# Eight-layer transformer on one core: set-up, first normalisation and small projections written as one program

## What is computed

```python
def _layernorm(x, axis=-1, eps=1e-05):
    m = jnp.mean(x, axis=axis, keepdims=True)
    v = jnp.var(x, axis=axis, keepdims=True)
    return (x - m) / jnp.sqrt(v + eps)

# first attention: query = _layernorm(x), key = value = ctx_4096
Q = query @ Wq + bq      # 512 x 512
K = key @ Wk + bk        # 512 x 128
V = value @ Wv + bv      # 512 x 128
...
x = x + _L0_xattn_ref(_layernorm(x, axis=-1), ctx_4096, ctx_4096, ...)
```

## Time and profile before

| what | value |
|---|---|
| median of 3 runs | 1848.16 us (1847.71 to 1848.89) |
| the profiled execution | 1848.91 us, of which the span of the trace is 1847.1 us |
| TensorE busy | 1687.6 us, 91% of the span |
| VectorE busy | 1205.1 us, 65% |
| ScalarE busy | 810.1 us, 44% |
| GpSimd busy | 1007.9 us, 55% |
| mean granted clock of TensorE | 0.958 of full speed |

### The profile page before, as it was taken

One profiled execution on the slowest core, in us unless ns is written; L12 is line 12 of the kernel. 1 busy time (PEld: TensorE's weight loads), 2 busy tenths in 40 slices (PEclk: granted clock), 3 DMA queues, 4 the chain that ended last, 5 costly groups with the idle time before them and its releaser, 6 DMA issues. The chain is left out here.

```text
span 1847.1 us, 27513 instructions
## 1 busy us (share of the span) xinstructions
PE 1687.6 (91%) x8898; PEld 1406.5 (76%) x8898; DVE 1205.1 (65%) x2393; ACT 810.1 (44%) x2591; POOL 1007.9 (55%) x1031
## 2 busy tenths in 40 slices
PE   3899967489999999999999999999999999997796
PEld 2777856368888888888788878888888888886684
DVE  5367665637777777766777775566655655554695
ACT  2088840134444444444344444444444444444342
POOL 2033320046666677766667676656656776662353
PEclk9989989599999999999999999999999999999896
DMA  3000010022222222221112222222222332220100
GB/s 132 24 1 1 0 40 1 26 68 64 69 58 64 69 69 77 67 57 58 52 57 59 62 80 75 58 69 75 63 67 72 90 93 70 79 75 6 59 18 29
DMA packets 57233, 104.10 MB, mean 56 GB/s; under 512 B 8016, under 2 KB 8528, under 8 KB 56976
## 3 DMA queue, kind: packets, MB, share of 16 engines
q1 hardware_dynamic: 55440, 99.27, 18.6%
q10 hardware_dynamic: 1664, 3.21, 0.5%
HBM read 100.36 MB, written 2.10 MB: 55 GB/s over the span
## 5 line engine op out<-in xcount | busy, mean ns | idle before, releaser
L891 POOL TENSOR_TENSOR a_probs<-a_probs,a_total 128x512 f32<-128x512 f32 x128 | 135.3, 1057 | 210.7 <-DVE a_total L1315 208.5
L83 POOL TENSOR_TENSOR a_w_lo<-a_raw,a_w_hi 128x512 fp32r<-128x512 f32 x186 | 240.5, 1293 | 14.9
L68 PE MATMUL ps<-a_wo_hi,a_oT_lo 128*128 128x512 f32 x544 | 225.1, 414 | 6.9 <-DVE a_oT_lo L83 5.4
L70 PE MATMUL ps<-a_wo_hi,a_oT_hi 128*128 128x512 f32 x544 | 213.7, 393 | 0.0
L69 PE MATMUL ps<-a_wo_lo,a_oT_hi 128*128 128x512 f32 x544 | 212.1, 390 | 0.0
L1152 ACT ACTIVATE a_v_hi<-ps 128x128 fp32r<-128x128 f32 x128 | 35.5, 278 | 359.3 <-PE ps L1000 359.3
L83 POOL TENSOR_TENSOR a_wo_lo<-a_raw,a_wo_hi 128x512 fp32r<-128x512 f32 x128 | 165.4, 1292 | 10.3
L1290 DVE TENSOR_TENSOR a_cross<-ps,a_cross 128x512 f32<-128x512 f32 x128 | 88.2, 689 | 120.1 <-ACT a_cross L1138 117.6
L1299 DVE SCALAR_TENSOR_TENSOR a_probs<-a_cross,a_q_scale,a_mask 128x128 f32<-128x128 f32 x256 | 156.4, 670 | 0.0
L83 DVE TENSOR_TENSOR a_pT_lo<-ps,a_pT_hi 128x512 fp32r<-128x512 f32 x192 | 128.4, 682 | 25.7 <-ACT a_pT_hi L2093 20.1
L1993 POOL TENSOR_TENSOR a_probs<-a_probs,a_total 128x1024 f32<-128x1024 f32 x32 | 60.8, 1899 | 153.5 <-DVE a_total L2149 153.5
(11 more groups left out here) (408 smaller groups left out, 5031.5 us busy)
## 6 DMA issues: line engine op xcount, KB each, us to landing
a_raw<-in_L_wq SPq DMA_DIRECT2D x128, 256.0 KB, 2.7
a_raw<-in_L_wo SPq DMA_DIRECT2D x128, 256.0 KB, 2.6
a_raw<-in_L_wkv SPq DMA_DIRECT2D x64, 256.0 KB, 2.6
a_raw<-in_L_main SPq DMA_DIRECT2D x12, 256.0 KB, 3.1
setup_raw<-in_cT SPq DMA_DIRECT2D x4, 512.0 KB, 7.1
x<-in_x ACTq DMA_DIRECT2D x8, 256.0 KB, 9.0
t_c_raw<-in_context SPq DMA_DIRECT2D x8, 256.0 KB, 5.7
out<-x SPq DMA_DIRECT2D x8, 256.0 KB, 2.0
```

The source lines that it names most:

```text
L68: pe.matmul(out, lhs_lo, rhs_hi, start=start, stop=False)
L70: return pe.matmul(out, lhs_hi, rhs_hi, start=False, stop=stop)
L83: return eng.tensor_tensor(out_lo, value, hi.bitcast(F32), ALU.subtract)
L891: pool.tensor_tensor(heads(probs[:, :]), heads(probs[:, :]), along_last(total[:, :], S), ALU.mult).then_inc(s["probs"], 1)
```

## The change

The set-up, the normalisation and the projections become one block, `prepare`, with one barrier behind it. In it:

- SP issues the key weights, the context, the value weights, three bias columns and the output bias, then the query weights. ScalarE's queue loads x.
- ScalarE rounds the context as before. VectorE makes its low half, then the statistics, one sequence after another as they arrive, and the moments; it adds epsilon itself. GpSimd splits all six weight chunks, with the power -0.5 after the fourth. VectorE then multiplies mean and scale to a shift.
- TensorE starts with the keys, tile by tile as the context's low halves come. The values are computed transposed (weights stationary, two products with 512 columns), given their bias by ScalarE, and turned by eight transposes; VectorE copies them out.
- ScalarE normalises the rows (scale and shift as column operands) and rounds them after the transposes; VectorE makes the low halves.
- The query products of the first four sequences alternate with the transposes of the last four; those of the last four sequences follow. VectorE empties them with the bias.
- GpSimd adds the output bias to x after all weights are split.

The caller changes with it:

```diff
-        set_up(nc, C, A["x"], A["cT"])
-        attention_small_heads(nc, C, A["L0_wkv"], A["L0_wq"], A["L0_wo"], A["L0_bk"], A["L0_bq"], A["L0_xattn_bv"],
-                              A["L0_xattn_bo"])
+        attention_small_heads(nc, C, A)
```

More of the change, by code:

```diff
@@ L170, in tiles_of @@
     return bank.rearrange("p (k t) -> p k t", k=KT)
[L175 to L214, removed]
 E = 8
@@ L1860, with prepare @@
 RW = RH * S
-def project_small_heads(nc, C, q32, k32, v32, wkv, wq, bk, bq, bv, bo):
+def prepare(nc, C, A, q32, k32, v32):
     with ExitStack() as ctx:
-        ph = Phase(nc, ctx, "p0")
-        xT = ph.split("xT", KT * B * S)
-        raw, w_s = ph.sb("raw", (2 + SETS) * CHUNK), ph.split("w", (2 + SETS) * CHUNK)
-        bk_col, bq_cols, bv_row = ph.sb("bk", 1), ph.sb("bq", SETS), ph.sb("bv", S)
-        s = ph.sems("w_in bias_in w_hi w_lo mm taken")
+        ph = Phase(nc, ctx, "p")
+        c_raw, w_raw, w_s = ph.sb("c_raw", KT * B * S), ph.sb("w_raw", (2 + SETS) * CHUNK), ph.split("w", (2 + SETS) * CHUNK)
+        xT, vT = ph.split("xT", KT * B * S), ph.sb("vT", B * S)
+        xn = [ph.sb(f"xn{p}", D) for p in (0, 1)]
+        stats, moments = ph.sb("stats", B * 6), ph.sb("moments", B * 2)
+        rstd, shift = ph.sb("rstd", B), ph.sb("shift", B)
+        bk_col, bv_col, bq_cols, bo_row = ph.sb("bk", 1), ph.sb("bv", 1), ph.sb("bq", SETS), ph.sb("bo", D)
+        s = ph.sems("zeroed const biases c_hi c_lo w_hi w_lo stats moments veps rstd shift xn xn_T x_hi x_lo biased"
+                    " mm k_taken vT_taken v_turned v_taken q_taken "
+                    + " ".join(f"x_in{b} " for b in range(B)) + " ".join(f"c_in{k}" for k in range(KT))
+                    + " " + " ".join(f"w_in{c}" for c in range(2 + SETS)))
@@ L1878, in chunk @@
+        number = {cp: n for n, cp in enumerate(products)}
+        block = ctx.enter_context(nc.Block())
         def chunk(tile, c):
             return tile[:, c * CHUNK:(c + 1) * CHUNK]
-        def load_weights(sp):
-            for c in range(2 + SETS):
-                src = wkv[c] if c < Q_CHUNK else wq[c - Q_CHUNK]
-                sp.dma_start(chunk(raw, c), src).then_inc(s["w_in"], 16)
-            sp.dma_start(bk_col[:, :], bk).then_inc(s["bias_in"], 16)
-            sp.dma_start(bq_cols[:, :], bq).then_inc(s["bias_in"], 16)
-            sp.dma_start(bv_row[:, :], bv.partition_broadcast(128)).then_inc(s["bias_in"], 16)
@@ new lines, in round_turned @@
+            def round_turned(b):
[5 more added lines that the diff above has]
+                act.activation(tile[:, blk(h, BANK)], banks[n % 4], ACT.Identity, bias=col[:, 0:1]).then_inc(s[sem], 1)
+            for b in range(B):
+                act.dma_start(C.x[:, blk(b, D)], A["x"][b]).then_inc(s[f"x_in{b}"], 16)
@@ new lines, in _ @@
+            for k in range(KT):
+                act.wait_ge(s[f"c_in{k}"], 16)
[8 more added lines that the diff above has]
+            take(vT, bv_col, V_CHUNK, 1, "vT_taken")
@@ L1914, in _ @@
+            for b in range(B):
+                round_turned(b)
+                if b + 2 < B:
+                    normed(b + 2)
         @block.vector
         def _(dve):
[L1916 to L1931 removed]
@@ L1946, in attention_small_heads @@
+            for n in range(SETS):
+                low_turned(HALF_B + n)
+                take_queries(n, 0)
+            for n in range(SETS):
+                take_queries(n, 1)
+def attention_small_heads(nc, C, A):
     with ExitStack() as ctx:
```

127 lines of the change are left out of this document (43 added, 84 removed).

## The result

The kernel with the change takes 1836.82 us (median of 5 runs, 1833.97 to 1839.65); the kernel before, run beside it, took 1848.89 (5 runs, 1847.71 to 1853.41). The ratio is 0.9933, with a 95% interval of 0.9920 to 0.9946: the kernel after is faster by 12 us, 0.7% and clear of the noise, where 19.0 us were forecast.

What follows compares the result with a forecast made beforehand. Three programs in a row, bound by transfers, by a VectorE-GpSimd-ScalarE chain and by TensorE, were to overlap: 81.1 - 61.9 - 0.2 = 19.0 us less, 1848.9 to 1829.9, or 1829.2 against the median; range 1824 to 1834.5.

Steps and rivals of the forecast that it cites:

- Front: Set-up transfers and context splitting: last low half ready at 15.5 us, with 1.3 for a weight chunk and 0.3 for GpSimd collisions.
- Keys and values: TensorE's first products: upper clock level from 20.5 us after a credit for early work, keys ending at 21.3, values at 26.8.
- Root and shift: Moments chain on VectorE and GpSimd: variance at 21.2 us, root 22.9, shift 23.7, with about a microsecond of cover.
- Rows: ScalarE normalising at 0.81 and rounding at 0.60, 1.41 us a row; the fourth low half opens the queries at 34.3.
- The fall of the clock: TensorE, nearly idle from 29.1 to 34.3 us, loses its upper level; queries then lose 2.1 us (1.6 to 2.9).
- Rival (a): No fall of the clock in the rows: 2.1 us come back, giving 1827.1 us; chance 0.27.
- Queries: Query products with row transposes and one round trip: 21.9 + 2.0 + 1.4 us, ending at 61.9 with clock loss and pipe's end.
- Barrier: The one barrier left clears 41 semaphores instead of 6 (0.76 us for 6): 0.2 us added, bounds 0 and 0.4.
- Sum: Gain before the attention's start: 81.1 - 61.9 - 0.2 = 19.0 us less.
- Rival (b): The front waits, through late context, a blocked low half or a delayed root: 1831 to 1835 us, middle 1833; chance 0.20.
- Rival (d): No gain: queue order makes keys wait for moments, or low clock at the attention's start gives it back; chance 0.02.
- a microsecond saved before the attention is one saved in the whole: Everything later waits for the attention's start at 82.66 us, so the 19.0 us carry over whole unless the clock takes them back.

Runs made afterwards that it cites:

- again: The kernel after, unedited, traced and timed once more beside the kernel before: 1837.23 us (5 runs), ratio 0.992.
- values_rows: Kernel after with values computed row by row as before, 96 multiplications of 128 columns and no transposes back: 1838.75 us (one run).
- pieces: Kernel after with the first four sequences' query products cut into pieces of 256 columns, so that queries begin sooner: 1833.86 us (4 runs), ratio 0.9898.
- rows_dve: Kernel after with rows normalised by VectorE instead of ScalarE, which then only rounds: 1831.70 us (one run).

## Why the prediction was right and wrong

- **Front.** Last low half of the context forecast at 15.5, measured 14.39 + 1.23 = 15.62. The collision with GpSimd went the other way: VectorE had started first (14.39 against 14.70) and kept its 1.23, and GpSimd's cast took 1.38 instead of the 0.62 of the earlier trace rows.
- **Keys and values.** The clock rose at 18.8 instead of 20.5, so the credit for the start was too small. Worth half of those 1.7 us, less 0.1 for the later front, it ends the keys at 20.7 (21.3) and the values at 26.4 (26.8).
- **Root and shift.** Variance at 21.6 (forecast 21.2), root 23.4 (22.9), shift 23.95 (23.7). But ScalarE took the shift up at 24.27 us, so the chain had 0.3 us of cover and not the 1.1 of the forecast (24.8 less 23.7). It was right that the shift hits a split: 0.56 us against 0.15 where GpSimd does not split.
- **Rows.** Pitch 1.19 us instead of 1.41: the sum of 0.81 and 0.60 counts an overlap twice, since ScalarE starts the next instruction 0.1 us before the end shown for the last (28.77 against 28.28 + 0.60). Queries open at 33.31 instead of 34.3.
- **The fall of the clock** was taken, and came, earlier (32.6) and for longer, 6.8 us. From 33.31 to 39.5 half is lost, 3.1 us instead of 2.1. In *again* the low stretch of the queries lasts only to 36. Rival (a), no fall, describes *values_rows* and three of the four profiles of *pieces*, not this kernel.
- **Queries.** 33.31 to 61.83 is 28.5, less 3.1 for the clock 25.4; forecast 25.3. Last product done at 61.83, forecast 61.9.
- **Barrier.** 1.01 us against 0.76; forecast +0.2.
- **Sum** 19.0; measured 19.03. Errors of a microsecond each way cancelled, the early rows against the longer fall. In *again* the attention starts at 62.09, 20.6 us earlier than before, so hitting 19.0 was luck.
- **Rival (b)** did not come about. **Rival (d)** had the right mechanism, the low clock after the attention's start, with the wrong place and size. I had looked at that stage's first rise alone (107.7), and behind the change it stood 20.5 us at the lower level instead of 23.9, a small gain (the lead grew there).

The step that failed is the sentence that a microsecond saved before the attention is one saved in the whole, and the sum built on it: 1848.9 less 19.0. The sentence has a condition, "unless the clock takes it back", and the sum puts that term at nothing. It takes two things as fixed that are not, the level of the kernel before and the length of the unedited part. The profiled execution before had the least time at the lower clock of fourteen traces, and the three runs shown, 1847.71 to 1848.89, lay at the low end of the 36 runs in the table, to which they belong: 1847.7 to 1857.1 with a mean of 1852.5, and only three of the other 33 at or below 1848.89. Against the kernel before run beside it the change is worth 12.1 us (the first time) and 15.4 (*again*). Of the 7.6 us by which the forecast missed, 4.1 are the later part of the profiled pair (1768.57 less 1764.44), 2.85 are the distance from the profiled run after to its median, and 0.7 the one that I had taken off for the median of before. Told in means over all repeated runs: the ten runs of the kernel after average 1837.2, 8.1 above the 1848.16 less 19.0. Of that 4.3 are the mean level of the kernel before (1852.5), 4.6 the longer later part, and −0.8 the stage, which saved 19.8 on the average of its two traces. The 4.6 is the cost that the prediction left out; some 3 of it are the clock, as estimated above, and the rest is open. The range had ±1 us for the attention and nothing for the 1700 us behind it; the scatter of the later part alone asks for some 5 us upwards. The last sign that I had named of being wrong, times beyond the attention's start that differ by over 3 us once shifted, is the one that appeared.

## What to carry to other kernels

Read an early stage's gain from the start of the first instruction behind it, where it can be told to a microsecond or two even from one trace; then ask how much the unedited rest scatters, and put that into the range. Where TensorE bounds a kernel with many gaps of 1 to 2 us, the same instructions take 0.5% more or less as its clock falls at some gaps or not, so three close runs and one trace need not show the baseline's level. A stage that makes TensorE wait a little in front of a long run of products pays twice, for the wait and for the clock: feeding it smaller pieces of work sooner (*pieces*) took away the wait, and the fall in three profiles of four.

## What the runs showed of the hardware

- The fall of TensorE's clock at a given gap is not settled by the program: at one place thirteen traces idled 0.96 to 1.41 us and show no fall, one idled 1.52 us and does, while in *again* it fell at other places and TensorE was busy 6.2 us longer. Whether the length of the gap decides it, one fall in fourteen does not show.
- A GpSimd cast beside a two-input VectorE operation took 1.38 us instead of 0.62, and the VectorE operation its usual 1.23. Small VectorE operations of 8 columns with one or two inputs took 0.54 and 0.56 us beside GpSimd's splitting (0.79 in *rows_dve*) and 0.15 to 0.17 without it.
- A multiplication of 512 columns starts 0.228 us after the one before it at the upper level, one of 256 columns 0.12 (*pieces*), one of 128 columns 0.11 (*values_rows*): from 256 to 128 columns almost nothing is won.
- ScalarE's alternating instructions of 0.81 and 0.60 us follow each other at 1.19 a pair, not 1.41.
